# Latent attention on one core: the last tile of the maxima pass ahead of the value matmuls, the low half of the probabilities on GpSimd, the high half multiplied first

## The reference, cut to what matters

```python
q_blhd = einsum('bld,dhk->blhk', x, Wq)            # 16 heads of 64
latent = einsum('bld,dc->blc', x, Wkv_down)        # 64 numbers per token
k_blhd = einsum('blc,chk->blhk', latent, Wk_up)
v_blhd = einsum('blc,chk->blhk', latent, Wv_up)
attn = einsum('bqhd,bkhd->bhqk', q_blhd, k_blhd) / sqrt(64)
attn = softmax(where(mask, attn, neg_inf), axis=-1)   # causal
y = einsum('bhqk,bkhd->bqhd', attn, v_blhd)
out = einsum('bqhd,hdo->bqo', y, Wout)
```

## Time and profile before

| | us |
|---|---|
| median of three runs | 3108.84 |
| the profiled execution's own time | 3109.72 |
| its span from the first to the last instruction | 3108.0 |
| TensorE busy | 2517.6 (81%) |
| VectorE busy | 2180.1 (70%) |
| ScalarE busy | 1427.3 (46%) |
| GpSimd busy | 842.7 (27%) |

### The profile page before, as it was taken

How to read it: one execution, slowest core, us unless ns; L and a number is a source line. 1 busy time by engine, 2 the same in 40 slices (tenths; PEclk the granted TensorE clock), 3 DMA queues, 4 the chain that set the end, 5 groups by cost and what they waited for, 6 DMA issues and landing times. The chain is left out here.

```text
span 3108.0 us, 38743 instructions
## 1 busy us (share of the span) xinstructions
PE 2517.6 (81%) x13889; PEld 1339.3 (43%) x13889; DVE 2180.1 (70%) x3910; ACT 1427.3 (46%) x2061; POOL 842.7 (27%) x820
## 2 busy tenths in 40 slices
PE   7967999899998999989678256688888888886256
PEld 3423444344443444444333134345555555554134
DVE  3597776757858688576970765488888878973765
ACT  5533354444544445444234111167667766774111
POOL 3323354443443444434133000002112211212000
PEclk9988999999999999999889578599999999998578
DMA  5000000000000000000000100000000000000101
GB/s 167 12 0 1 1 1 1 1 1 1 1 1 1 1 1 1 1 1 1 1 1 18 42 1 27 9 1 2 2 2 3 2 3 1 2 2 14 47 0 55
DMA packets 29460, 33.08 MB, mean 11 GB/s; under 512 B 6568, under 2 KB 25704, under 8 KB 29272
## 3 DMA queue, kind: packets, MB, share of 16 engines
q1 hardware_dynamic: 28296, 28.02, 2.9%
q0 software_dynamic: 976, 2.56, 0.3%
HBM read 25.72 MB, written 4.19 MB: 10 GB/s over the span
## 5 line engine op out<-in xcount | busy, mean ns | idle before, releaser
L661 POOL TENSOR_TENSOR g_lo<-g_full,g_hi 128x512 f16<-128x512 f32 x512 | 660.5, 1292 | 1024.6 <-ACT g_hi L727 1019.3
L727 ACT ACTIVATE g_full<-hid,b_col 128x512 f32<-128x512 f32 x512 | 352.7, 689 | 627.6 <-PE hid L152 625.9
L150 PE MATMUL acc<-g_hi,w_hi 128*128 128x512 f16 x1024 | 394.4, 385 | 58.2 <-POOL g_lo L661 58.2
L150 PE MATMUL hid<-y_hi,w_hi 128*128 128x512 f16 x1024 | 396.2, 387 | 25.0 <-DVE y_lo L715 20.9
L151 PE MATMUL acc<-g_lo,w_hi 128*128 128x512 f16 x1024 | 395.1, 386 | 0.0
L152 PE MATMUL acc<-g_hi,w_lo 128*128 128x512 f16 x1024 | 394.9, 386 | 0.0
L151 PE MATMUL hid<-y_lo,w_hi 128*128 128x512 f16 x1024 | 394.9, 386 | 0.0
L152 PE MATMUL hid<-y_hi,w_lo 128*128 128x512 f16 x1024 | 394.0, 385 | 0.0
L727 ACT ACTIVATE g_hi<-hid,b_col 128x512 f16<-128x512 f32 x512 | 350.0, 684 | 0.0
L1975 DVE TENSOR_REDUCE mla_m_col<-mla_ps 128x1 f32<-128x512 f32 (+3 forms) x512 | 224.9, 483 | 60.4 <-PE mla_ps L1817 54.7
L2078 ACT ACTIVATE mla_p_full<-mla_ps 128x1280 f32<-128x1280 f32 x128 | 158.4, 1237 | 138.9 <-PE mla_ps L1847 138.5
(11 more groups left out here) (368 smaller groups left out, 4737.1 us busy)
## 6 DMA issues: line engine op xcount, KB each, us to landing
stage<-in_L_ffn_w_dram SPq DMA_DIRECT2D x16, 512.0 KB, 5.0
x<-in_L_attn_x_dram SPq DMA_DIRECT2D x8, 512.0 KB, 8.6
routed_w<-in_L_ffn_w_dram SPq DMA_DIRECT2D x4, 1024.0 KB, 8.1
out_dram<-x SPq DMA_DIRECT2D x8, 512.0 KB, 5.7
mla_sums<-mla_sum_row SPq DMA_DIRECT2D x128, 2.0 KB
mla_wq<-in_L_attn_Wq_dram SPq DMA_DIRECT2D x1, 1024.0 KB, 7.4
mla_wout<-in_L_attn_Wout_dram SPq DMA_DIRECT2D x1, 1024.0 KB, 9.7
routed_wqkv<-in_L_ffn_wq_dram SPq DMA_DIRECT2D x2, 256.0 KB, 3.6
```

The costliest lines, as they stand in the source:

```text
L150: pe.matmul(out, w_hi, v_hi, start=first, stop=False)
L661: pool.tensor_tensor(g_lo[:, g, :], g_full[:, g, :], g_hi[:, g, :], ALU.subtract).then_inc(tail_done, 1)
L727: act.activation(out[:, g, :], hid[:, ht % 4, :], ACT.Gelu, bias=b1_col[:, ht:ht + 1], scale=1.0 / WS).then_inc(gelu_done, 1)
```

## The change

Three things are moved. The exponentials are written in the order `p_hi`, `p_full`, each with a semaphore of its own. The subtraction that makes `p_lo` goes from VectorE to the head of GpSimd's step. TensorE's value matmuls are split in two passes over the four tiles: first both products with `p_hi` after a wait for `p_head`, then the product with `p_lo` after a wait for `p_tail`. And the untransposed scores of tile 1 go from behind the value matmuls to just behind the transposed scores; VectorE takes their maximum right behind the other three. The arithmetic is the same.

```diff
--- before.py
+++ after.py
@@ -1752,7 +1752,8 @@
         m_out = sem("m_out")
         m_put = [sem(f"m_put{i}") for i in range(2)]
         st_done = sem("st_done")
-        exp_done = sem("exp_done")
+        p_head = sem("p_head")
+        p_whole = sem("p_whole")
         p_tail = sem("p_tail")
         pv_done = sem("pv_done")
         pv_out = sem("pv_out")
@@ -1832,7 +1833,7 @@
             hb, hh, hn = head_of(b, h + 1)
             if exists(hb):
                 if not isinstance(hn, int) or hn > 0:
-                    pe.wait_ge(exp_done, 2 * hn)
+                    pe.wait_ge(p_whole, hn)
                 if hh % GROUP_HEADS == 0:
                     g = hh // GROUP_HEADS
                     pe.wait_ge(q_tail, hn + GROUP_HEADS)
@@ -1846,6 +1847,12 @@
                               q_lo[:, hh % RING, t * P:], start=False, stop=False)
                     last = pe.matmul(flat[:, at:at + P], ident_b[:, :], block_k[:, :], start=False, stop=True)
                 last.then_inc(st_done, 1)
+
+
+            hb, hh, hn = head_of(b, h + LEAD - 2)
+            if exists(hb):
+                pe.wait_ge(s_max, TILES * hn + 1)
+                query_scores(pe, (slot + (h + LEAD - 2) // H) % 2, hh, QUERY_TILES[-1]).then_inc(s_rest, 1)
 
 
             if exists(before) and OUTPUT_AT <= h < OUTPUT_AT + TILES:
@@ -1910,7 +1917,7 @@
 
 
             if exists(b):
-                pe.wait_ge(p_tail, n + 1)
+                pe.wait_ge(p_head, n + 1)
                 if h == 0:
                     pe.wait_ge(val_out, 2 * (b + 1))
 
@@ -1920,20 +1927,16 @@
                     pe.wait_ge(scaled, MLA_PAIRS * before + h - SPREAD_AT)
                 if exists(before) and OUTPUT_AT < h <= OUTPUT_AT + TILES:
                     pe.wait_ge(x_added, TILES * before + h - OUTPUT_AT)
+                own_cols = [slice(KEY_AT[t], KEY_AT[t] + SEQ - t * P) for t in range(TILES)]
                 for t in range(TILES):
-                    out = ps[:, own_bank, t * P:]
-                    cols = slice(KEY_AT[t], KEY_AT[t] + SEQ - t * P)
-                    hi, lo = p_hi[:, h % 2, cols], p_lo[:, h % 2, cols]
+                    out, hi = ps[:, own_bank, t * P:], p_hi[:, h % 2, own_cols[t]]
                     pe.matmul(out, val_hi[:, slot, t, :], hi, start=(t == 0), stop=False)
-                    pe.matmul(out, val_hi[:, slot, t, :], lo, start=False, stop=False)
-                    last = pe.matmul(out, val_lo[:, slot, t, :], hi, start=False, stop=(t == TILES - 1))
+                    pe.matmul(out, val_lo[:, slot, t, :], hi, start=False, stop=False)
+                pe.wait_ge(p_tail, n + 1)
+                for t in range(TILES):
+                    last = pe.matmul(ps[:, own_bank, t * P:], val_hi[:, slot, t, :], p_lo[:, h % 2, own_cols[t]],
+                                     start=False, stop=(t == TILES - 1))
                 last.then_inc(pv_done, 1)
-
-
-            hb, hh, hn = head_of(b, h + LEAD - 2)
-            if exists(hb):
-                pe.wait_ge(s_max, TILES * hn + 1)
-                query_scores(pe, (slot + (h + LEAD - 2) // H) % 2, hh, QUERY_TILES[-1]).then_inc(s_rest, 1)
 
 
             hb, hh, hn = head_of(b, h + LEAD)
@@ -1984,6 +1987,8 @@
                 dve.wait_ge(s_done, hn + 1)
                 for t in QUERY_TILES[:-1]:
                     query_maxima(dve, hh, t)
+                dve.wait_ge(s_rest, hn + 1)
+                query_maxima(dve, hh, QUERY_TILES[-1])
 
 
             if exists(before) and SPREAD_AT <= h < SPREAD_AT + MLA_PAIRS:
@@ -2045,18 +2050,6 @@
                 dve.tensor_tensor(val_lo[:, 1 - slot, :, 0:LATENT], src, val_hi[:, 1 - slot, :, 0:LATENT],
                                   ALU.subtract).then_inc(val_out, 1)
 
-            hb, hh, hn = head_of(b, h + LEAD - 2)
-            if exists(hb):
-                dve.wait_ge(s_rest, hn + 1)
-                query_maxima(dve, hh, QUERY_TILES[-1])
-
-            hb, hh, hn = head_of(b, h + 1)
-            if exists(hb):
-                dve.wait_ge(exp_done, 2 * (hn + 1))
-                dve.tensor_tensor(p_lo[:, hh % 2, :], p_full[:, hh % 2, :], p_hi[:, hh % 2, :],
-                                  ALU.subtract).then_inc(p_tail, 1)
-
-
             hb, hh, hn = head_of(b, h + LEAD)
             if exists(hb) and h % 2 == 0:
                 for i in range(2):
@@ -2074,9 +2067,9 @@
             hb, hh, hn = head_of(b, h + 1)
             if exists(hb):
                 act.wait_ge(st_done, hn + 1)
-                for out in (p_full, p_hi):
+                for out, made in ((p_hi, p_head), (p_full, p_whole)):
                     act.activation(out[:, hh % 2, :], flat[:, 3 * 512:3 * 512 + KEY_COLS], ACT.Exp,
-                                   scale=float(MLA_DIM) ** -0.5).then_inc(exp_done, 1)
+                                   scale=float(MLA_DIM) ** -0.5).then_inc(made, 1)
             if exists(after) and h in TURN_AT:
                 k = TURN_AT.index(h)
                 act.wait_ge(y_turned, KD * after + k + 1)
@@ -2103,6 +2096,11 @@
         def pool_step(pool, b, slot, h):
 
             before, after = b - 1, b + 1
+            hb, hh, hn = head_of(b, h + 1)
+            if exists(hb):
+                pool.wait_ge(p_whole, hn + 1)
+                pool.tensor_tensor(p_lo[:, hh % 2, :], p_full[:, hh % 2, :], p_hi[:, hh % 2, :],
+                                   ALU.subtract).then_inc(p_tail, 1)
             if exists(after) and h == NORM_AT:
                 pool_variance(pool, norm_step, NORM_STEPS * after + TILES, stats, ln_col, norm_const,
                               var[:, :], minus_half[:, :])
```

## The result

The changed kernel takes 3207.86 us (median of four, 3204.82 to 3208.79) against 3109.61: a ratio of 1.0315, 95% interval [1.0297, 1.0333], 98 us slower. The profiled execution took 3208.14 us, span 3205.6.

The account below looks back on a forecast made before the run. TensorE, 86% busy and nearly full, was taken as the bound, with about 90 us of waits to win. 3109.7 (profiled execution) + 52 stalls + 31 clock = 3193, 3192 against the median; range 3135 to 3238.

Parts of the forecast that it names:

- its two terms: Over the whole stream: +52 us from longer pairs of steps (stalls), and +31 us from TensorE's lowered clock behind stalls.
- `p_lo` off VectorE wins nothing on the path: Taking 128 subtractions, 205.4 us, off VectorE gains nothing: even steps wait for ScalarE, odd ones delay only unawaited work.
- The rival in which VectorE is the bound by load: Odd step's stall: relieved VectorE finishes tile 3's maximum before TensorE needs it; some 60 us won, 3050; chance of faster 0.05.
- `p_lo` on GpSimd takes 2.8, in time: GpSimd's subtraction runs from S+2.65 to S+5.45 (S: transposed scores done), before TensorE wants it at S+6.2 or later.
- The first copy is held up: VectorE's first query copy of a pair waits for GpSimd's `p_lo`, ending at S+5.59 instead of S+4.60, 0.99 late.
- the forecast sign, every second copy near 1.3: In the profile after, every second L2066 query copy on VectorE would take near 1.3 us instead of 0.29.
- The rival in which the copies go free: GpSimd does not hold the query copies; plain pairs take 10.9, total 3118; chance 0.08, two thirds of it slower.
- The waiting copy goes ahead of `o_lo`: In spread steps the waiting copy goes before GpSimd's `o_lo`; the second copy stands behind `o_lo`, 0.27 more.
- The rival that GpSimd goes straight on: GpSimd starts `o_lo` first; in steps 4, 6, 8, 10 the copy waits 1.1 longer: +23, 3215; chance 0.20.
- Tile 1's wait in front of the values: In odd steps TensorE waits from S+5.00 to about S+8.15 for tile 3's maximum; a plain pair is 1.7 longer.
- The clock: Slow TensorE stretches, 1.2 to 1.7 us each, follow half of six long stalls a batch: +31 us, bounds nothing to +70.
- The rival in which the clock holds: The stalls come on TensorE but no slow stretches follow: +50, 3160; chance 0.17.

Follow-up runs that it names:

- t4: Changed kernel plus seven 512-column matmuls (1.5 us) in each odd step ahead of the wait for tile 3's maximum: 3156.02 us, ratio 1.0149 to the kernel before.
- t2: Changed kernel with tile 1 put back behind the value matmuls, low half still on GpSimd: 3147.31 us, ratio 1.0115 to the kernel before.
- u1: Kernel before with only tile 1 moved, low half on VectorE, plus seven filling matmuls in odd steps: 3121.83 us, ratio 1.0045.
- u3: Changed kernel with GpSimd's low half in even steps held until both query copies are through, plus seven filling matmuls in odd steps: 3140.15 us, ratio 1.0106.
- e7: Changed kernel with the exponentials in their old order and the value matmuls in one pass: 3208.19 us, ratio 1.0327 to the kernel before.
- t3: Changed kernel with GpSimd's low half in even steps held until both query copies are through: 3156.12 us, ratio 1.0148 to the kernel before.
- e9: e8 with the low half made by VectorE again in steps 4, 6 and 8: 3077.22 us, ratio 0.9888 to the kernel before.
- e8: Changed kernel; queries behind the maxima in steps 0-3 and 10-15, tile 1 behind the values in 4-9, inverse in step 2: 3102.13 us, ratio 0.9968.

## Why the prediction was right

The direction, the mechanism and the size held: 3192 forecast, 3208 measured, the range 3135 to 3238. The total is closer than its two terms: the stalls came out 6 us below the forecast and the clock 21 above it, and part of that cancels. The pairs of steps of a full batch show how well the stalls were counted. For each kernel the least of six batches stands here, read from the ends of the transposed scores:

| steps | before | forecast | t4 (changed, idle time filled) | changed |
|---|---|---|---|---|
| 0, 1 | 11.13 | 11.9 | 11.72 | 11.81 |
| 2, 3 | 10.82 | 12.1 | 11.89 | 11.89 |
| 4, 5 | 12.24 | 12.8 | 12.52 | 14.03 |
| 6, 7 | 12.45 | 12.8 | 12.50 | 12.51 |
| 8, 9 | 14.41 | 14.2 | 14.64 | 14.64 |
| 10, 11 | 12.88 | 14.75 | 14.43 | 14.43 |
| 12, 13 | 14.64 | 15.75 | 15.72 | 15.72 |
| 14, 15 | 12.71 | 13.55 | 13.51 | 13.51 |

In steps 4 and 5 the changed kernel has a low stretch in every batch. Its plain pair, steps 12 and 13 of the first batch, takes 5.00 and 8.33 where 5.0 and 6.9 stood in the forecast; in t4, without the low stretch, 5.00 and 6.65.

Point by point:

- *`p_lo` off VectorE wins nothing on the path.* Held: t2, with VectorE relieved, is slower than before, and u1 and u3 have the same plain pair whichever engine makes the low half. The rival in which VectorE is the bound by load is out.
- *`p_lo` on GpSimd takes 2.8, in time.* 2.61: the straight line through the two sizes (2.60) was right and my choice 0.19 too long. In time: e7 shows that order and passes bring nothing.
- *The first copy is held up.* Held, but in fewer places and for less time than the forecast sign, every second copy near 1.3. Of the 128 copies 19 take 1.05 to 1.10, less than 1.28 since GpSimd is done sooner; they lie in the first batch and in steps 0 and 2 of the others. 20 take 0.58, in the spread steps, where `q_hi` comes later; there the first copy had mostly taken 0.64 to 0.81 already before, behind `o_lo`. In steps 8, 12 and 14 of a full batch they keep 0.29. The rival in which the copies go free is out, by t3 and u3.
- *The waiting copy goes ahead of `o_lo`.* Held: in spread steps the first copy takes 0.58 and ends with `p_lo`, and the second takes 0.41, so it is the second that stands behind `o_lo`. The rival that GpSimd goes straight on is out. Step 4 of the second batch in the changed kernel, GpSimd and then VectorE:

```profile
2175.39 2.61 POOL L2102 TENSOR_TENSOR mla_p_lo<-mla_p_full,mla_p_hi 128x1280 f16<-128x1280 f32 x1 [2.35 <-ACT mla_p_full L2071]
2177.96 1.20 POOL L2113 TENSOR_TENSOR mla_o_lo<-mla_o,mla_o_hi 128x512 f16<-128x512 f32 x1
```
```profile
2177.57 0.58 DVE L2059 COPY mla_q_hi<-mla_q_hi 64x512 f16<-64x512 f16 x1 [2.14 <-ACT mla_q_hi L2093]
...
2178.89 0.41 DVE L2059 COPY mla_q_hi<-mla_q_hi 64x512 f16<-64x512 f16 x1
```

- *Tile 1's wait in front of the values.* Held: 61 waits, in odd steps, up to 3.5. With the clock out of the way (t4) a full batch takes 107.0 against 101.4 before (a batch without a low stretch), +5.6, forecast +6.5; over the stream +46, forecast +52. Forecast were six stalls of 2.6 to 3.4 a batch and two of 1.8; as a rule five of 2.3 to 2.8 came, one of 3.5 in step 9, and two of 1.6.
- *The clock* is the term that was mis-sized: +31 forecast, +52 measured. I took low stretches behind half of the six long stalls, and that share was the error: 38 of the 48 stalls of 2.0 us or more were followed by one, where the forecast amounts to some 20 to 25 in the stream. The price of each, 1.2 to 1.7, was right: 52 us for 34 stretches less is 1.5. The rival in which the clock holds is out; t4 shows what it would have been, 3156, near the 3160 given for it.
- *Not in the forecast*: the casts of step 8 and the scaling of the inverse, held up as the copies are. They are in the measured 46. Steps 8 and 9 are the only pair that came out longer than forecast, 14.64 against 14.2; the others are shorter, and so the sum hid it.

## What to carry to other kernels

Before work goes from a busy engine to an idle one, ask which instruction ends last ahead of the bound engine; if it waits for a third engine and not for the work that is moved, nothing is won. Here a GpSimd instruction of 2.6 us delayed the short copies, casts and scalings of VectorE from SBUF to SBUF that came while it ran, so what counted was when it ran (e9 against e8), not how busy GpSimd was. And a wait moved ahead in an in-order queue takes all behind it along: here the stalls of 2.3 to 3.5 us cost as much again in clock, 52 us beside 46.

## What was not expected of the hardware

A VectorE tensor_scalar of 64 columns, 0.20 us, took up to 2.33 beside GpSimd's subtraction of 1280 columns, and a cast of 0.41 took 2.84, while reductions and two-operand operations with one operand in PSUM kept their time (the queries' low half 0.68 to 0.69 under GpSimd too). A two-operand scaling with both operands in SBUF did not: 0.23 became 2.53 in e8. And 448 useless matmuls made a kernel 52 us faster: filling the idle time kept the granted clock at 0.99 instead of 0.92.
